# Attention experts of a fused graph network: value projections by rank inside the passes instead of in a row, and the last expert's second layer in two halves

## What is computed

```python
# 128 tokens, D = 512, E = 8 experts, K = 2 per token, H = 8 heads of 64, F = 64
keys = x @ gate_Wk.T + gate_bk
probs = softmax(einsum('bsd,ed->bse', keys, expert_queries) * D ** -0.5)
gated = probs * (one_hot of the top 2);  gated /= gated.sum
def _expert(x, ...):
    q, k, v = split(x @ Wqkv.T + bqkv, 3)
    attn = softmax(q * scale @ k.T)            # per head, over all 128 tokens
    ctx = (attn @ v) @ Wo.T + bo
    x = layernorm(x + ctx, g1, be1)
    h = gelu(gelu(x @ W1.T + bf1) @ W2.T + bf2)  # 512 -> 64 -> 512, exact gelu
    return layernorm(x + h, g2, be2)
out = sum over experts of gated[expert] * _expert(x)
```

## Time and profile before

| | before |
|---|---|
| median of 3 runs | 435.19 us |
| the profiled execution, its own time | 435.27 us |
| its span, first to last instruction | 433.6 us |
| TensorE busy | 401.1 us (93%) |
| VectorE busy | 197.3 us (45%) |
| ScalarE busy | 128.7 us (30%) |
| GpSimd busy | 47.2 us (11%) |
| mean granted TensorE clock | 0.988 of full |

### The profile page before, as it was taken

How to read it: one execution, slowest core, us unless ns; L and a number is a source line. 1 busy time by engine, 2 the same in 40 slices (tenths; PEclk the granted TensorE clock), 3 DMA queues, 4 the chain that set the end, 5 groups by cost and what they waited for, 6 DMA issues and landing times.

```text
span 433.6 us, 7726 instructions
## 1 busy us (share of the span) xinstructions
PE 401.1 (93%) x2854; PEld 295.0 (68%) x2854; DVE 197.3 (45%) x575; ACT 128.7 (30%) x381; POOL 47.2 (11%) x101
## 2 busy tenths in 40 slices
PE   7998999896588989999999998998999999999996
PEld 6698665796077869997455655665688994493482
DVE  4844545555995244401324558687733531201102
ACT  2313312514453102332300564462113232122130
POOL 4000010010364000011002122011100000000000
PEclk9999999999689999999999999999999999999999
DMA  8999359449002000899998555851920599999900
GB/s 287 383 427 353 122 203 411 163 191 389 3 2 70 29 0 26 310 392 299 374 334 323 182 166 130 303 183 62 400 98 2 226 423 421 421 419 421 384 2 24
DMA packets 19721, 101.44 MB, mean 234 GB/s; under 512 B 3639, under 2 KB 5559, under 8 KB 8804
## 3 DMA queue, kind: packets, MB, share of 16 engines
q1 hardware_dynamic: 19396, 100.94, 61.0%
q10 hardware_dynamic: 288, 0.02, 0.0%
HBM read 100.68 MB, written 0.26 MB: 233 GB/s over the span
## 4 chain that ended last, share of the span: by engine, by line
PE 72%; DVE 12%; issue 7%; ACT 3%; POOL 3%; DVEq 2%; POOLq 0%; ACTq 0%
PE ps L1251 13%; PE ps L1237 12%; PE ps L1636 7%; PE ps L1919 6%; PE ps L1664 4%; PE ps L1220 3%; PE ps L1730 2%; PE ps L1398 2%; PE ps L1653 2%; PE ps L1228 1%; PE ps L1726 1%; PE ps L1985 1%; PE ps L1435 1%; PE ps L1350 1%; PE ps L1271 1%
## 5 line engine op out<-in xcount | busy, mean ns | idle before, releaser
L1220 PE MATMUL ps<-ident 128*128 128x128 f32 x350 | 48.5, 291 | 2.8 <-POOL ident L690 2.8
L1220 PEld LDWEIGHTS ps<-ident 128*128 128x128 f32 x350 | 45.5, 204 | 5.3 <-POOL ident L690 2.8
L1251 PEld LDWEIGHTS ps<-y_t,ew 128*128 128x128 f32 x352 | 39.9, 192 | 1.7 <-issue 1.7
L1251 PE MATMUL ps<-y_t,ew 128*128 128x128 f32 x352 | 40.2, 275 | 0.0
L1636 PE MATMUL ps<-y_t,ew 128*128 128x128 f32 x256 | 29.2, 276 | 0.0
L1636 PEld LDWEIGHTS ps<-y_t,ew 128*128 128x128 f32 x256 | 28.8, 192 | 0.0
L2449 DVE COPY dense<-ps 128x512 f32<-128x512 f32 x8 | 5.5, 692 | 43.7 <-PE ps L1237 43.7
L1237 PE MATMUL ps<-ew,y_t 128*128 128x512 f32 x56 | 25.1, 596 | 0.0
L2731 DVE SCALAR_TENSOR_TENSOR t<-prob_store 128x512 f32<-128x512 f32 x6 | 4.2, 692 | 36.4 <-ACT prob_store L1154 20.4
L867 ACT ACTIVATE prob_store<-ps,nmax_s 128x128 f32<-128x128 f32 x48 | 16.9, 381 | 10.6 <-DVE nmax_s L2111 10.5
L1237 PEld LDWEIGHTS ps<-ew,y_t 128*128 128x128 f32 x56 | 10.2, 190 | 12.0 <-issue 11.8
(11 more groups left out here) (545 smaller groups left out, 755.7 us busy)
## 6 DMA issues: line engine op xcount, KB each, us to landing
ew<-in_l_w SPq DMA_DIRECT2D x20, 1024.0 KB, 21.4
dense<-in_l_w SPq DMA_DIRECT2D x12, 1024.0 KB, 20.8
ew<-in_l_wk SPq DMA_DIRECT2D x8, 1024.0 KB, 9.7
ew<-in_l_wq SPq DMA_DIRECT2D x7, 1024.0 KB, 6.1
ew<-in_l_wv SPq DMA_DIRECT2D x6, 1024.0 KB, 8.9
ew<-in_l_wo SPq DMA_DIRECT2D x5, 1024.0 KB, 4.9
ew<-in_gqa_wq SPq DMA_DIRECT2D x3, 1024.0 KB, 10.8
ew<-in_gqa_wk SPq DMA_DIRECT2D x3, 1024.0 KB, 15.4
```

The source lines that it names most:

```text
L1220: pe.matmul(ps[:, b, 3 * P:4 * P], ident[:], ident[:], start=True, stop=True)
L1251: last = pe.matmul(ps[:, b, m * n:(m + 1) * n], w[:, c, (first + m) * P:(first + m + 1) * P], in_t[:, c, 0:n], start=(c == 0), stop=(c == ...
```

## The change

The values are projected by rank instead of by number, each straight into the tile that its step reads: v0 where it was, v1 ahead of the probabilities of step 0, v2 inside pass 0, v3 and v4 inside pass 1, v5 and v6 inside pass 2, v7 inside pass 3. Five of the last six stand in two pieces, with other matmuls between. `values_copy` and its eight copies on GpSimd go, and with them `v_all`, so that slots 12 and 13 take weights. All value weights are now loaded by rank, so that none is issued before `l2_order` is known. VectorE's copies move to the places where their projections are done. v0 now uses bank 2, the bank of the last key projection, and waits for `l2_k_ready`. Three `keep_clock` calls go. `step_h2` stands ahead of `probs_t`. The last expert's second layer is two matmuls of 256 columns in banks 7 and 0, and its gelu, its sum and its statistics are two halves each. ScalarE's list is otherwise as before.

```diff
...
-L2_LOADS = (*(("k", e, e) for e in range(E)), ("v", 0, 8), ("v", 1, 9), ("v", 2, 0), ("v", 3, 1),
...
+L2_LOADS = (*(("k", e, e) for e in range(E)), ("q", 0, 8), ("v", 0, 9), ("q", 1, 12), ("q", 2, 13),
+            ("o", 0, 0), ("q", 3, 1), ("q", 4, 2), ("v", 1, 3), ("v", 2, 4), ("o", 1, 5), ("o", 2, 6), ("q", 5, 8), ("q", 6, 7),
+            ("v", 3, 9), ("v", 4, 12), ("o", 3, 13), ("o", 4, 0), ("q", 7, 1), ("v", 5, 2), ("v", 6, 3), ("o", 5, 4),
+            ("o", 6, 5), ("v", 7, 6), ("o", 7, 7), ("gcn", 0, 8), ("gcn", 1, 9), ("gcn", 2, 12))
+V_BANKS = (2, 7, 1, 2, 1, 2, 1, 2)
...
-            sp.wait_ge(*at("peer_q_projected", 2))
-            load_l2("v", 0, 0)
             sp.wait_ge(*at("residual_summed", 8))
-            load_l2("v", 1, 1)
+            sp.wait_ge(*at("exph_v_projected", 1))
...
             sp.wait_ge(*at("l2_order_ready", 1))
             e0 = expert_at(0)
-            sp.wait_ge(*at("l2_k_projected", 3))
             load_l2("q", 0, e0)
+            load_l2("v", 0, e0)
+            e1, e2 = expert_at(1), expert_at(2)
+            load_l2("q", 1, e1)
+            load_l2("q", 2, e2)
+            sp.wait_ge(*at("l2_k_projected", 1))
+            load_l2("o", 0, e0)
...
-            def values_copy(t):
-                pool.wait_ge(*at("l2_v_ready", E))
-                if t:
-                    pool.wait_ge(*at("l2_attended", t))
-                for a, p in enumerate(L2_STEPS[t]):
-                    pool.tensor_copy(values_of[a], v_all[:, bass.ds(experts[p], 1), :].rearrange("p e n -> p (e n)")) \
-                        .then_inc(sig(f"l2_v_copied{t}"), 1)
...
-                    act.wait_ge(*at("l2_h2_projected", t + 1))
-                    nc.scalar.activation(h2_of[t], bank(7), ACT.Gelu).then_inc(sig("l2_h2_ready"), 1)
+                    halves = range(2 if t == LAST else 1)
+                    for half in halves:
+                        act.wait_ge(*at("l2_h2_projected", t + half + 1))
+                        n = D // len(halves)
+                        nc.scalar.activation(h2_of[t][:, half * n:(half + 1) * n], ps[:, (7, 0)[half], 0:n], ACT.Gelu) \
+                            .then_inc(sig("l2_h2_ready"), 1)
...
-            def expert_v(e):
-                l2_landed("v", e)
-                if e == 1:
-                    pe.wait_ge(*at("l2_k_ready", E))
-                if e >= 2:
-                    pe.wait_ge(*at("l2_v_ready", e - 1))
-                project((7, 2)[e % 2], y_t, l2_w("v", e)).then_inc(sig("l2_v_projected"), 1)
+            def expert_v(p, chunks=range(CH)):
+                if 0 in chunks:
+                    l2_landed("v", p)
+                    pe.wait_ge(*at("l2_v_ready", p - 1) if p > 1 else at("l2_k_ready", E))
+                for c in chunks:
+                    last = project_term(V_BANKS[p], y_t, l2_w("v", p), c)
+                if CH - 1 in chunks:
+                    last.then_inc(sig("l2_v_projected"), 1)
...
             def step_attend(t, b):
-                pe.wait_ge(*at(f"l2_v_copied{t}", len(L2_STEPS[t])))
+                pe.wait_ge(*at("l2_v_ready", L2_STEPS[t][-1] + 1))
...
+                elif t == LAST:
+                    for half, b in enumerate((7, 0)):
+                        last = pe.matmul(ps[:, b, 0:D // 2], h1_t[:], ew2[:, half * D // 2:(half + 1) * D // 2],
+                                         start=True, stop=True)
...
                 pair_q(t + 2)
+                if t:
+                    expert_v(L2_STEPS[t + 1][0])
                 x1_transposes(t)
                 turn_q(t + 2)
+                expert_v(L2_STEPS[t + 1][1], (0, 1))
                 step_h1(t)
+                expert_v(L2_STEPS[t + 1][1], (2, 3))
+                step_h2(t)
                 probs_t(t + 1)
-                step_h2(t)
                 step_scores(t + 2)
...
             expert_v(0)
             step_scores(0)
+            gather_rows(1)
+            pair_q(1)
+            turn_q(1)
             expert_v(1)
-            gather_rows(1)
-            expert_v(2)
-            pair_q(1)
-            expert_v(3)
-            turn_q(1)
             probs_t(0)
-            for e in range(4, E):
-                expert_v(e)
             step_scores(1)
...
             step_attend(2, 1)
-            keep_clock(2, times=2)
+            expert_v(5, (0,))
             step_o(2)
+            expert_v(5, (1, 2, 3))
             expert_q(4)
             x1_transposes(2)
+            expert_v(6, (0, 1))
+            step_h1(2)
+            expert_v(6, (2, 3))
+            step_h2(2)
+            probs_t(3)
+            step_scores(4)
+
+            step_attend(3, 1)
+            expert_v(7, (0,))
+            step_o(3)
+            expert_v(7, (1, 2, 3))
             turn_scatter()
...
-            step_attend(3, 1)
-            keep_clock(2, times=2)
-            step_o(3)
-            keep_clock(2, times=2)
             probs_t(4)
...
-            def v_copy(e):
-                dve.wait_ge(*at("l2_v_projected", e + 1))
-                dve.tensor_copy(v_all[:, e, :], bank((7, 2)[e % 2])).then_inc(sig("l2_v_ready"), 1)
+            def v_copy(p):
+                dve.wait_ge(*at("l2_v_projected", p + 1))
+                second = any(step[1:] == (p,) for step in L2_STEPS)
+                dve.tensor_copy(values_of[second], bank(V_BANKS[p])).then_inc(sig("l2_v_ready"), 1)
...
+                if t == LAST:
+                    for half in range(2):
+                        r = slice(half * D // 2, (half + 1) * D // 2)
+                        dve.wait_ge(*at("l2_h2_ready", t + half + 1))
+                        dve.tensor_tensor(h2_of[t][:, r], x1_of[t][:, r], h2_of[t][:, r], ALU.add)
+                        settle()
+                        dve.bn_stats(half_st[:, 6 * half:6 * half + 6], h2_of[t][:, r])
+                    return
...
```

More of the change, by code:

```diff
@@ L391, in build @@
         l2_order = sb("l2_order", [P, E], U32)
-        k_all, v_all = (dense[:, s:s + 2, :].rearrange("p s (e n) -> p (s e) n", n=D) for s in (2, 4))
+        k_all = dense[:, 2:4, :].rearrange("p s (e n) -> p (s e) n", n=D)
         k_second = sb("k_second", [P, CH, P])
@@ L544, in _ @@
             load_g2_rows(1, (e1, e2))
-            e3, e4 = expert_at(3), expert_at(4)
+            sp.wait_ge(*at("l2_k_projected", 6))
+            load_l2("o", 1, e1)
+            e5, e6, e7 = (expert_at(p) for p in (5, 6, 7))
             sp.wait_ge(*at("l2_k_projected", 7))
-            load_l2("v", 5, 5)
+            load_l2("o", 2, e2)
             sp.wait_ge(*at("l2_q_projected", 1))
-            load_l2("v", 6, 6)
+            load_l2("q", 5, e5)
             sp.wait_ge(*at("l2_k_projected", 8))
-            load_l2("v", 7, 7)
+            load_l2("q", 6, e6)
@@ L574, in _ @@
-            load_l2("o", 5, e5)
             sp.wait_ge(*at("l2_x1_ready", 2))
             load_l2_rows(2, (e3, e4))
+            sp.wait_ge(*at("l2_q_projected", 3))
+            load_l2("q", 7, e7)
+            load_l2("v", 5, e5)
             sp.wait_ge(*at("l2_h2_projected", 1))
             load_l2_small(1, (e1, e2))
-            sp.wait_ge(*at("l2_q_projected", 3))
-            load_l2("o", 6, e6)
+            sp.wait_ge(*at("l2_v_projected", 3))
+            load_l2("v", 6, e6)
+            load_l2("o", 5, e5)
@@ L769, in residual_rows @@
                 pool.wait_ge(*at("l2_rows_landed0", rows_value))
-                pool.tensor_tensor(erows[:, 0, BO, :], erows[:, 0, BO, :], y[:], ALU.add).then_inc(sig("l2_residual_ready"), 1)
+                pool.tensor_tensor(erows[:, 0, BO, :], erows[:, 0, BO, :], y[:], ALU.add).then_inc(sig(f"l2_residual_ready{t}"), 1)
             def inner_norm(t, which):
@@ L1761, in step_h2 @@
                                          start=True, stop=True)
+                elif t == LAST:
+                    for half, b in enumerate((7, 0)):
+                        last = pe.matmul(ps[:, b, 0:D // 2], h1_t[:], ew2[:, half * D // 2:(half + 1) * D // 2],
+                                         start=True, stop=True)
+                        if half == 0:
+                            last.then_inc(sig("l2_h2_projected"), 1)
                 else:
@@ L2608, in _ @@
             weights_max(0)
-            v_copy(1)
-            weights(0, (0,))
-            v_copy(2)
-            weights(0, (1,))
-            v_copy(3)
+            weights(0)
             pair_q_bias(1)
             prob_t_copy(0)
-            for e in range(4, E):
-                v_copy(e)
             weights_max(1)
             v_bias(0)
+            v_copy(1)
             first_sums(0)
@@ L2645, in _ @@
             weights(3)
+            v_copy(5)
             keep_pair(1)
-            dve.wait_ge(*at("l2_gates_turned", 1))
-            dve.tensor_copy(gated_t[:], ps[0:E, 1, 3 * P:4 * P])
-            dve.tensor_copy(scatter, ps[:, 1, 0:3 * P]).then_inc(sig("l2_scatter_ready"), 1)
+            v_copy(6)
             prob_t_copy(3)
@@ L2659, in _ @@
             first_norm(3)
+            v_copy(7)
```

(3 more changed lines are left out.)

76 lines of the change are left out of this document (28 added, 48 removed), and 3 rows, old and new, of the table L2_LOADS.

## The result

The changed kernel took 436.82 us (median of 20 runs, 434.92 to 438.23) beside 435.17 us for the kernel before (20 runs, 434.85 to 436.16). The ratio is 1.0042, with an interval of 1.0031 to 1.0053: slower by 0.4%, where 435.4 and no measurable change were forecast.

What follows compares the result with a forecast made beforehand. TensorE's list was taken to set the end. Added 6.3 us, removed 5.8 and 0.3 at the last expert, sum +0.2: 435.5 against the profiled execution, 435.4 us on the median's scale, range 434.0 to 436.9.

Steps and rivals of the forecast that it cites:

- v0: Start of the value projections: v0, now in bank 2, waits for the last key's bias on ScalarE, +1.38 us.
- the hole: Before the queries of step 1: TensorE idles until ScalarE copies the gathered rows after eight exps, +3.56 us.
- the transposes: Behind the queries of step 1: their transposes wait for ScalarE's copy of the query rows, +0.75 us.
- the pieces: v2 to v7 in 11 pieces instead of 3 runs: 8 extra handovers of 0.07, +0.6 us, bounds 0 to 1.2.
- idle time: TensorE's waits in the passes, 4.64 us in all, get projections in front of them: -3.8 us.
- the fillers: Three filler calls in the passes are removed: -2.0 us.
- The term for the last expert: Last expert's second layer, gelu, sum and statistics in halves: -0.3 us, between 0 and -0.6.
- the one on the clock: Hole before step 1's queries: shorter than four idle microseconds that left the clock up, so no term in the sum.
- The rival by the clock: Clock falls in the hole before step 1's queries and stays down 6 us: up to 2.5 more, 437.9 us; chance 0.1.
- the faster rival: Pieces hand over for nothing (-0.6) and all idle time in the passes is filled (0.8 more): 434.0 us; chance 0.2.
- No weight came late: Rival: a weight ranked late, or waits at the swapped second layer, gives 436.3 to 436.5 us; chance 0.15.
- no change: Whole kernel: gains and losses even out as summed, within about 0.2%; chance 0.5, 0.51 in the final numbers.

Runs made afterwards that it cites:

- e1_fill: Changed kernel plus thirteen unused filler matmuls between the gather and the queries of step 1; 435.12 us, ratio 0.9992 to the kernel before.
- e7_layer_whole: e6_all_covered with the last expert's second layer, gelu, sum and statistics whole again, as before the change; 429.60 us.
- e4_v0_bank7: Changed kernel with v0 back in bank 7 and v1 in bank 2, so v0 waits only for its weights; 435.46 us, ratio 0.9995.
- e3_v1_first: Changed kernel with v1 moved ahead of the gather and the probabilities' transposes ahead of those of the queries; 432.69 us, ratio 0.9938.
- e5_copy_first: Changed kernel with ScalarE's copy of the gathered rows put ahead of the eight exps of step 0; 432.35 us, ratio 0.9928.
- e10_before_hole: Kernel before the change, with only v1, v2 and v3 moved behind the transposes of the queries of step 1; 441.83 us, ratio 1.0146.
- e6_all_covered: Changed kernel with ScalarE's copy ahead of the exps, v0 in bank 7, and v1 in three pieces in the holes; 429.57 us, ratio 0.9867.

## Why the prediction was wrong

**The sum was near, and is what the kernel does when the clock stays up.** 435.4 was forecast; the lowest group of the changed kernel is near 435.0, and e1_fill, with every wait and piece of the change in it, takes 435.12. Three terms came true one by one: v0 1.32 for 1.38, the hole 3.44 for 3.56, the transposes 0.70 for 0.75. The passes went from 60.82 to 75.84 us. Six projections of 3.46 moved into them, 20.8, so they gained 5.7 net of the pieces; 5.8 - 0.6 = 5.2 was forecast. Of it 4.64 - 0.82 = 3.8 is idle time, as forecast. With 2.0 for the fillers only some 0.1 is left for the pieces and all else, less than the 0.6 of the sum. As v2's cut alone reads 0.2, something was saved elsewhere in the passes, and these rows do not say where. The term for the last expert was too large: 0.29 of its 0.3 is there at the aggregate, but e7_layer_whole shows 0.07 of it at the next matmul and nothing in the runs. These two misses are of opposite sign, so part of the agreement is luck. With the measured terms the sum is 1.32 + 3.44 + 0.70 - 5.74 - 0.07 = -0.35, and e1_fill lies 435.46 - 435.12 = 0.34 below the median of the kernel before that was measured with it.

**The step that failed** is the one on the clock: "The new hole is shorter than the four idle microseconds that left the clock up, so the sum has no term for it." I read from 106 to 110 us, idle with the clock at 1.00, that four idle microseconds do no harm. These four are part of a longer idle stretch, and the rows leave out where the clock fell (kernel before; first the matmul that ends the stretch, then columns as in the earlier trace rows):

```profile
113.03 5.93 PE L1553 MATMUL ps<-dense,eq_t 128*8 128x512 f32 x8 [7.30 <-ACT big L966]
```

```profile
110.00:111.00 1.00, 0.00 (x0) 0.00 (x0) 1.00 (x6) 0.00 (x0) 0.00 (x0) 0.98 0.00 0
111.00:112.00 1.00, 0.00 (x0) 0.00 (x0) 1.00 (x5) 0.52 (x2) 0.00 (x0) 0.50 0.00 0
```

TensorE was idle for 7.30 us, and the clock fell at about 111, while it still was. That it was up until 110 was also the luck of one execution. The same idle stretch is in every trace of this case, and over 109 to 110 us the clock was at 1.00 in two of the fourteen and at 0.50 to 0.97 in the others. The profile of the changed kernel has 0.91 over the four microseconds that were the bound:

```profile
106.00:110.00 4.00, 0.00 (x0) 0.00 (x0) 3.96 (x16) 2.13 (x5) 1.24 (x2) 0.91 0.00 2
```

Nor does a clock of 1.00 at the end of an idle stretch promise anything for the work behind it: it was 1.00 through 209 to 210 in the changed kernel too, and fell after the queries had begun. The trace of before had a warning for shorter holes as well, in the next two stretches:

```profile
118.00:124.00 6.00, 3.72 (x25) 2.52 (x24) 6.00 (x28) 4.02 (x13) 3.78 (x6) 1.00 0.01 3
124.00:128.00 4.00, 4.00 (x23) 4.00 (x23) 4.00 (x19) 1.91 (x7) 2.47 (x4) 0.58 0.01 2
```

TensorE was busy for 3.72 of the 6.00 us from 118 to 124, with idle times of 1.72 and 0.55 us, and behind them, busy throughout, it had 0.58 of its clock from 124 to 128. What the runs showed in place of the missing term is nothing in 5 of 34 runs, some 1.8 us in 20 and 3.0 in 9. The hole wanted a term with both ends, nothing and the 2.5 us that I had worked out.

**The rival by the clock** had the right mechanism and place, at a chance of 0.1; times above the lowest group came in 29 of 34 runs. Its price of 2.5 lay between the two upper groups, 1.8 and 3.0 above the lowest: in the middle group the clock was down for some 3.4 us and not for 6. Its condition, a hole of more than four microseconds or one that counts together with the wait before v0, fell: 3.4 us was enough, with that wait (the changed kernel) and without (e4_v0_bank7), and 2.1 us was enough in six of twelve runs; at 1.0 us and less (e1_fill, e3_v1_first, e5_copy_first) no group split off in 21 runs. The Trainium skill (TensorE: Matmul & The Clock Gate, section "Why this matters for your kernels") warns of just this, and the trace agrees, with 0.50 granted from 212 to 215 us.

**The rivals that did not come.** The gains in the passes were 0.5 larger than summed, nearly the 0.6 that the faster rival gave to the pieces, but 0.82 of idle time was left unfilled, and a lowest group near 435.0 is not 434.0. No weight came late, and no wait stands at the swapped second layer but 0.3 at the last weighted sums, where 0.2 stood.

**What the chances missed:** the range, 434.0 to 436.9, holds the median with 0.1 to spare, which is luck: it was meant to leave the clock's price out, and the third group lies outside. The chances put 0.51 on no change, because a kernel with more than one outcome was treated as one outcome with a small risk.

## What to carry to other kernels

Work moved off a place to fill idle time elsewhere uncovers what it was covering: look at what the other engines do in that place, in the order of their lists, and reorder them with the move. Here one copy put ahead of eight exps, v0 left in its old bank, and v1 in three pieces in the holes turned 0.4% slower into 1.3% faster, with the rest of the change as it was. A new idle hole on TensorE carries two prices, its length and a lower clock on the matmuls behind it; where the trace has no hole of that size, both ends belong into the sum. A stretch cut out of a longer wait is no such hole: read on to where the wait ends. And a kernel whose runs fall into narrow groups should be read by group: the median of a mixture says little about any of them.

## What was not expected of the hardware

The clock's outcome differs from run to run of one program: with the same 2.1 us hole, six runs were near 435 us and six were not. So does the moment of its fall. In the changed kernel it was full through the idle time and 0.50 from 212 us on, when the matmuls had been running for about a microsecond. In e10_before_hole it was down when the queries began at 209.15:

```profile
209.00:210.00 1.00, 0.85 (x5) 0.26 (x9) 0.00 (x0) 0.00 (x1) 0.00 (x0) 0.51 1.00 418
```

And fillers counted for one timing hold back a matmul when the work ahead of it gets faster: 0.34 us after its operand in e6_all_covered, 0.14 with two fillers fewer.
